# Layer norms: variance and root of a batch laid out as four quarters of its tokens, 138 columns wide

## What is computed

```python
def _layernorm(x, axis=-1, eps=1e-05):
    m = jnp.mean(x, axis=axis, keepdims=True)
    v = jnp.var(x, axis=axis, keepdims=True)
    return (x - m) / jnp.sqrt(v + eps)
...
h = h + _L0_attn_ref(_layernorm(h, axis=-1), ...)
h = h + _L0_ffn_ref(_layernorm(h, axis=-1), ...)
h = h + _L1_attn_ref(_layernorm(h, axis=-1), ...)
h = h + _L1_ffn_ref(_layernorm(h, axis=-1), ...)
```

## Time and profile before

| | us |
|---|---|
| median of 3 runs (2139.62 to 2151.6) | 2144.09 |
| the profiled execution | 2146.77 |
| its span in the trace | 2144.9 |
| VectorE, 20 reciprocals of the norms, busy | 71.4 |
| TensorE / VectorE / ScalarE / GpSimd busy | 1558.1 / 1316.5 / 745.3 / 720.1 |

### The profile page before, as it was taken

How to read it: one execution, slowest core, us unless ns; L and a number is a source line. 1 busy time by engine, 2 the same in 40 slices (tenths; PEclk the granted TensorE clock), 3 DMA queues, 4 the chain that set the end, 5 groups by cost and what they waited for, 6 DMA issues and landing times. The chain is left out here.

```text
span 2144.9 us, 31340 instructions
## 1 busy us (share of the span) xinstructions
PE 1558.1 (73%) x9132; PEld 1091.4 (51%) x9132; DVE 1316.5 (61%) x2105; ACT 745.3 (35%) x1369; POOL 720.1 (34%) x758
## 2 busy tenths in 40 slices
PE   5679999998601006766647548888888758999998
PEld 3457777775301004555534333333333456888787
DVE  3845555555477891111115777877777547989988
ACT  2245555554200002222203346667766321111111
POOL 1345555552000015777754012322221112323322
PEclk8689999999855556888767889999999858999999
DMA  4050000000210002444352000000000000000000
GB/s 136 0 230 1 0 0 0 0 0 0 84 21 0 1 0 60 73 68 77 70 120 66 4 2 2 0 0 0 0 0 0 1 32 7 12 11 15 11 15 14
DMA packets 69696, 60.85 MB, mean 28 GB/s; under 512 B 15789, under 2 KB 63675, under 8 KB 68363
## 3 DMA queue, kind: packets, MB, share of 16 engines
q1 hardware_dynamic: 52174, 47.52, 7.0%
q0 software_dynamic: 15744, 11.85, 3.9%
q10 hardware_dynamic: 1728, 0.85, 0.1%
HBM read 35.06 MB, written 25.18 MB: 28 GB/s over the span
## 5 line engine op out<-in xcount | busy, mean ns | idle before, releaser
L1609 DVE TENSOR_SCALAR at_clip<-at_slot 128x548 bf16<-128x548 f32 (+1 forms) x320 | 226.3, 722 | 79.0 <-PE at_slot L1452 72.2
L1540 ACT ACTIVATE at_clip<-at_slot,at_four 128x548 bf16<-128x548 f32 (+1 forms) x320 | 226.6, 713 | 126.3 <-PE at_slot L1452 124.5
L1452 PE MATMUL at_slot<-at_qm,at_ks 128*128 128x274 bf16 (+1 forms) x1280 | 216.4, 285 | 55.5 <-ACT at_clip L1540 45.4
L1590 POOL TENSOR_SCALAR at_qm<-at_qs,at_headmask 128x548 bf16<-128x548 bf16 x128 | 97.3, 780 | 359.5 <-DVE at_qs L1618 359.5
L1187 DVE TENSOR_SCALAR ex_y<-ex_ps_y,ex_rows 128x128 f32<-128x128 f32 (+1 forms) x96 | 29.2, 346 | 246.5 <-PE ex_ps_y L1134 246.0
L1452 PEld LDWEIGHTS at_slot<-at_qm,at_ks 128*128 128x128 bf16 (+1 forms) x1280 | 90.5, 97 | 150.3 <-ACT at_clip L1540 90.7
L1092 POOL DMA_INDIRECT moe_sums<-ex_y,slot_sums x80 | 125.0, 1563 | 54.4 <-DVE ex_y L1187 32.6
L467 PE MATMUL ga_kv<-ga_kern,ga_v 128*128 128x274 f32 x512 | 132.1, 400 | 14.8 <-ACT ga_kern L552 14.1
L2041 DVE TENSOR_REDUCE mx_routed<-mx_weighted 128x128 f32<-128x1024 f32 x69 | 137.6, 1994 | 2.4
L612 POOL TENSOR_TENSOR ga_rot<-ga_by_cos,ga_by_sin 128x274 f32<-128x274 f32 (+1 forms) x96 | 70.3, 732 | 165.7 <-DVE ga_by_sin L656 165.7
L1133 PE MATMUL ex_ps_y<-ex_down,ex_hid 128*128 128x128 f32 (+3 forms) x576 | 114.1, 357 | 12.5 <-ACT ex_hid L1174 12.5
(11 more groups left out here) (346 smaller groups left out, 3798.4 us busy)
## 6 DMA issues: line engine op xcount, KB each, us to landing
moe_sums<-ga_zeros SPq DMA_DIRECT2D x8, 1152.0 KB, 18.9
ar_rows<-moe_sums SPq DMA_DIRECT2D x32, 256.0 KB
ex_down<-in_down SPq DMA_DIRECT2D x32, 192.0 KB, 2.4
out_h<-H SPq DMA_DIRECT2D x22, 192.0 KB, 1.9
H<-in_text SPq DMA_DIRECT2D x1, 4096.0 KB, 20.7
token_rows<-tr_rows SPq DMA_DIRECT2D x16, 256.0 KB
patches<-in_patches SPq DMA_DIRECT2D x1, 1728.0 KB, 7.6
ga_sin<-in_sin SPq DMA_DIRECT2D x1, 1644.0 KB, 10.1
```

What stands on the lines that cost most here:

```text
L1452: last = nc.tensor.matmul(slot[SLOT[T % 2][u]][0:rows_of(t), s, 0:HALF], ks[p][:, t * P:t * P + rows_of(t)], qm[p][:, h, j * HALF:(j + 1) ...
L1540: nc.scalar.activation(clip[T % 2][u][0:r], slot[SLOT[T % 2][u]][0:r, :, 0:HALF], ACT.Relu, bias=four[0:r], scale=-1.0).then_inc(by_act, 1)
L1590: last = nc.gpsimd.tensor_scalar(qm[p][:, h, :], qs[:], headmask[:, h:h + 1], 1.0, ALU.mult, ALU.mult)
L1609: nc.vector.tensor_scalar(clip[T % 2][u][0:r], slot[SLOT[T % 2][u]][0:r, :, 0:HALF], 4.0, None, ALU.min).then_inc(by_dve, 1)
```

## The change

The variance matmul of a group is done in four quarters of the tokens (138, 136, 138 and 136 columns). Its weights for quarter j are 1/128 in columns 8j to 8j + 7 and zero elsewhere, and the four are summed in one PSUM region, so that quarter j lies on 8 of the group's 32 partitions. Root, reciprocal and both parts then work on 128 x 138 in place of 128 x 548. The broadcast picks row 32g + 8j for quarter j: four quarters x two parts, eight matmuls of 138 or 136 columns. `mean32` becomes `mean_rows` (128 x 4 x 32), `pick_row` becomes 128 x 4 x 128.

```diff
+QUART = 138
+QUARTERS = [(0, QUART), (QUART, HALF - QUART), (HALF, QUART), (HALF + QUART, HALF - QUART)]
...
-        rstd = [sb(f"rstd{v}", [P, 2, HALF], F32) for v in range(nv)]
+        rstd = [sb(f"rstd{v}", [P, QUART], F32) for v in range(nv)]
...
-        var_ps = ps("var", [P, 2, 512])
+        var_ps = ps("var", [P, 512])
...
-                    for j in range(2):
-                        last = nc.tensor.matmul(var_ps[32 * g:32 * g + 32, j, 0:HALF], k["mean32"][:],
-                                                sq[g][:, j * HALF:(j + 1) * HALF], start=True, stop=True)
+                    for j, (at, n) in enumerate(QUARTERS):
+                        last = nc.tensor.matmul(var_ps[32 * g:32 * g + 32, 0:n], k["mean_rows"][:, j, :],
+                                                sq[g][:, at:at + n], start=j == 0, stop=j == 3)
...
-                    for j in range(2):
+                    for j, (_, w) in enumerate(QUARTERS):
+                        to = bc_ps[n][:, j // 2, j % 2 * QUART:j % 2 * QUART + w]
                         for part in range(2):
-                            last = nc.tensor.matmul(bc_ps[n][:, j, 0:HALF], k["pick_row_r"][32 * g:32 * g + 32, :],
-                                                    rstd_parts[v][part][32 * g:32 * g + 32, j, :], start=part == 0, stop=part == 1)
+                            last = nc.tensor.matmul(to, k["pick_row_r"][32 * g:32 * g + 32, j, :],
+                                                    rstd_parts[v][part][32 * g:32 * g + 32, 0:w], start=part == 0, stop=part == 1)
...
-                    nc.scalar.activation(rstd[v][:], var_ps[:, :, 0:HALF], ACT.Sqrt, bias=eps[v][:], scale=a).then_inc(std_done, 1)
+                    nc.scalar.activation(rstd[v][:], var_ps[:, 0:QUART], ACT.Sqrt, bias=eps[v][:], scale=a).then_inc(std_done, 1)
...
-    a["mean32"] = np.full((P, 32), 1.0 / P, f)
-    a["pick_row"] = np.where(np.arange(P)[:, None] % 32 == 0, 1.0, 0.0).astype(f) * np.ones((1, P), f)
+    a["mean_rows"] = np.broadcast_to((np.arange(32)[None] // 8 == np.arange(4)[:, None]) / P, (P, 4, 32)).astype(f)
+    a["pick_row"] = np.broadcast_to((np.arange(P)[:, None] % 32 == 8 * np.arange(4)[None])[:, :, None], (P, 4, P)).astype(f)
```

More of the change, by code:

```diff
@@ L96, in layernorm @@
         sq = [sb(f"square{g}", [P, S], F32) for g in range(NGRP)]
-        rstd = [sb(f"rstd{v}", [P, 2, HALF], F32) for v in range(nv)]
-        rstd_parts = [[sb(f"rstd{v}{part}", [P, 2, HALF], F32R) for part in range(2)] for v in range(nv)]
+        rstd = [sb(f"rstd{v}", [P, QUART], F32) for v in range(nv)]
+        rstd_parts = [[sb(f"rstd{v}{part}", [P, QUART], F32R) for part in range(2)] for v in range(nv)]
         eps = [sb(f"eps{v}", [P, 1], F32) for v in range(nv)]
         xc_ps = [ps(f"centred{j}", [P, 512]) for j in range(2)]
-        var_ps = ps("var", [P, 2, 512])
+        var_ps = ps("var", [P, 512])
         bc_ps = [ps(f"bcast{j}", [P, 2, 512]) for j in range(2)]
@@ L269, in load_inputs @@
         block = st.enter_context(nc.Block())
-        consts = [("center", "center"), ("mean32", "mean32"), ("pick_row", "pick_row"), ("cols", "cols"),
+        consts = [("center", "center"), ("mean_rows", "mean_rows"), ("pick_row", "pick_row"), ("cols", "cols"),
                   ("ident", "ident"), ("W1", "W1"), ("W2", "W2"), ("same_expert", "same_expert"),
@@ L2081, in build @@
         H = sb("H", [P, NTP])
-        k = {"center": sb("center_sb", [P, P]), "mean32": sb("mean32_sb", [P, 32]), "pick_row": sb("pick_row_sb", [P, P]),
-             "pick_row_r": sb("pick_row_r", [P, P], F32R),
+        k = {"center": sb("center_sb", [P, P]), "mean_rows": sb("mean_rows_sb", [P, 4, 32]), "pick_row": sb("pick_row_sb", [P, 4, P]),
+             "pick_row_r": sb("pick_row_r", [P, 4, P], F32R),
              "cols": sb("cols_sb", [P, NCOLS]), "ident": sb("ident_sb", [P, P]), "W1": sb("W1_sb", [P, 5 * P]),
```

## The result

| | before | changed |
|---|---|---|
| median, 20 runs each, us | 2146.10 | 2154.38 |
| span of the profiled run, us | 2144.9 | 2151.2 |

The ratio is 1.0037, 95% interval 1.0027 to 1.0047: 8.3 us slower by the medians, where 18 us faster was forecast. By the 0.5% named ahead it counts as no change; the interval shows that it is a real, small loss.

The account below looks back on a forecast made before the run. No engine is full in the norms, so the order of waits decides; VectorE paces the first. -12 (first norm) - 6.6 (others) + 0.6 (loading) = -18 us, giving a 2126 us median, range 2110 to 2140.

Parts of the forecast that it names:

- the variance at 0: Variance matmuls in all norms: columns equal, doubled 32-column loads just hide; 0 added, bounds 0 and 0.2 us a batch.
- the third rival: Variance loses its four-fold overlap if look-ahead is under 48; extreme +45 us, 2171 us; decides from +1.8 a batch; chance 0.05.
- the broadcast: Each group's eight matmuls for four, paced by weight loads: +0.35 us at clock 1.0, +0.7 at 0.5; bounds 0 and 0.7.
- The price of a load: Broadcast weight load of 128 columns before a short matmul: 0.21 us at clock 0.5, 0.105 us at 1.0.
- chain: Reciprocal and two parts on VectorE in each norm: 4.8 us becomes 1.55 with gaps; only the bare part counts.
- root: Root on ScalarE at the loop's start: 0.72 us becomes 0.25, bounds 0.18 and 0.40; saves 0.9 us first norm, 0.4 others.
- loading: Loading stage: two constants grow by 192 and 48 KB at 391 GB/s, +0.6 us.
- the first rival: Broadcast's extra loads cost nothing, slipping under the matmul before: 12.6 us less, 2114 us; chance 0.12.
- the clock: Norms: waiting stretches go, so TensorE's granted clock, 0.73 in the first norm, rises; all at 1.0 gives -16 us there.
- The forecast's middle, -12 us: First norm: saving taken as the middle between -7.6 us at the present clock pattern and -16 at clock 1.0.
- the -7.6 of the old clock pattern: First norm with clock unchanged: -2.3 - 0.5 - 0.5 for the steps and -4.3 after the last batch.
- The "-4" for the other norms at full clock: Second to fourth norm, each: -4 us all at high clock, -1.3 at the present clock; -2.2 taken.

Follow-up runs that it names:

- the run with the first pair interleaved: Changed kernel with variance by quarter, plus groups 0 and 1 of variant 0's broadcast interleaved by quarter: 2132.8 us, norms 211.5 us.
- the run that has it alone: Kernel before with root, reciprocal and parts on the first 138 columns only, matmuls as before: norms 194.6 us, whole kernel 2158.6 us.
- the variance's order mended: Changed kernel with variance matmuls ordered quarter outside, group inside, after all four groups' waits: 2132.0 us, ratio 0.9941 to the kernel before; norms 215.7 us.
- the halves' run: Changed kernel's idea with two halves of 274 columns in place of four quarters: 2117.0 us, ratio 0.9872 to the kernel before; norms 199.8 us.

## Why the prediction was wrong, step by step

- **Failed: the variance at 0, bounds 0 and 0.2 us a batch.** The argument was that columns stay equal and loads hide. Both are true (interleaved, the 32 passes take 1.15 us), and the overlap went all the same: 2.62 us a batch in place of 1.27. The row showed four passes a group in a row and an overlap over them, and I asked only whether loads and columns fit. It cost 19.7 us (235.3 against 215.7). This is the third rival's mechanism, which had 0.05. Its worst case was all 32 passes in a row and 45 us; a reach of four passes delays each group by only four passes, 0.50 us, three times a batch. At 1.2 us a batch (19.7 / 16) the loss stayed under the +1.8 at which that rival was said to decide, and still took more than the 18 us of the forecast. That "no row shows a limit at 24" read the overlap as reaching over 24 queued instructions. It reached group by group, each into reach as the one before it started.
- **The rule of the Trainium skill beside it did not hold here.** TensorE: Matmul & The Clock Gate ("The mechanism") has a reorder window of 64 instructions, in which weight loads are pulled ahead, and has matmuls start strictly in program order. In these runs group 1's passes start before group 0's last ones (515.71 against 515.82 to 516.05 us), and only four passes ahead.
- **Mis-sized: the broadcast.** +0.35 us a group at full clock was right for the first group: its multiply comes 1.35 us after its broadcast began (515.01 - 513.66), where 1.02 + 0.35 were forecast, and the loads are 0.11 us apart. The second group of a pair was taken as side by side with the first; it starts 0.51 us late, with group 0's fifth pass, as in the variance. So a pair takes 1.62 us where about 1.2 were counted, of which the run with the first pair interleaved gave 4.2 us back in the norms. The price of a load held: the forecast halved the 0.21 us read at half clock, and in the changed kernel the passes of a group are 0.11 us apart at full clock and 0.21 at half.
- **Right: chain, root, loading.** Chain 1.6 us forecast 1.55; reciprocal 1.01 forecast 1.0; root 0.38 within its bounds of 0.18 and 0.40 but not at the 0.25 taken; loading +0.75 us forecast +0.6. The worth of the chain shows in the run that has it alone, 33 us; the first rival, which had no cost for the broadcast, came to 30 us by the same terms.
- **Half wrong: the clock.** The waits for the chain went, and in the other norms the clock rose from 0.82 and 0.85 to 0.89 and 0.93. In the first norm it stayed: 0.74 after, 0.73 to 0.76 in the runs that gain there. The forecast's middle, -12 us, had half of the way to full clock in it. With the variance's order mended the first norm comes to 74.0 us, 7.8 below 81.8, and with the first pair mended too to 72.7, 9.1 below: nearer the -7.6 of the old clock pattern. The "-4" for the other norms at full clock is not the sum of the terms named with it, which give some -2.3; the -2.2 taken is near what the mended kernel shows, -2.4 a norm (138.8 us in all three against 146.0).
- **The balance.** For the norms alone -18.6 us were forecast and +7.6 came. 19.7 are the variance's order and 4.2 the first pair's. The 2.3 that are left are the first norm, 2.9 short of its -12, less 0.6 that the others gave above their -6.6. With the variance mended the whole kernel stands at -13.4 us, with the first pair mended too the norms at -16.3. That this is near the forecast is in part luck: the term for the clock was too large, and in the mended kernel the second pair of a step still has its late start.

## What to carry to other kernels

Small matmuls in separate row or column strips of the array ran side by side here only when they were near each other in the instruction order: put the strip in the inner loop, and count how many passes one strip has in a row before the next one comes. When an engine's chain is shortened by spreading its data over more partitions, count what the spreading adds on TensorE, in weight loads as in columns, and ask how much shortening the cover beside the chain needs; a chain of 2.7 us in place of 4.8 gave 28 of the 33 us that one of 1.6 gives, at no matmul more. A cost bounded by "the columns are the same" is not bounded as long as the order changes.

## What was not expected of the hardware

- The reach of the out-of-turn start is four passes, counted in passes (a float32 matmul is two, a float32r one is one): eight float32 passes of 138 columns a group delay the next group by 0.50 us, six by 0.265 us, eight float32r passes of the broadcast by 0.51 us. Four in a row delay it by 13 to 15 ns. Whether passes or their weight loads are counted is not told apart, since each pass here has its own load.
- With all four groups as neighbours the 32 passes take 1.15 us, where the 16 passes of twice the columns took 1.27 us in the earlier trace rows and 1.4 in the halves' run. From first to last start it is 0.87 against 0.88 us; the rest is the last pass's own length. Shorter passes side by side cost nothing in themselves.
- A cast on 138 columns took 1.05 us in place of 0.23 in six of 16 steps (1.06 is the maximum in the tile view above). Those six lay beside a GpSimd square, as the subtraction of 1.57 us did before, and the ten others did not. But in the kernel before one subtraction lay wholly beside a square (1178.64 us) and took its usual 0.73. What delays it was not tried.
